# A bidirectional scan and a binary matmul on one core: stores at the end of late steps, whole low halves, and four small scalings moved

## The reference, cut to what matters

```python
# x, k: (4, 1024, 1024) float32; k serves as key and value; cond: (4, 256); weight: (1024, 1024)
tf = sigmoid(sum(cond, -1))[:, None, None]
decay = exp(-exp(w))[None, :] * (0.5 + 0.5 * tf[:, :, 0])
ek = exp(minimum(k, 30)); ekv = ek * k
# over time, forward and then in reverse:
#   a = a * decay + ekv[t] (nf, nb);  b = b * decay + ek[t] (df, db)
euk = exp(minimum(u + k, 30))
num = nf + nb - ekv + euk * k
den = df + db - ek + euk
y = sigmoid(x) * (num / maximum(den, 1e-8)) * (0.8 + 0.2 * tf)
bw = where(weight >= 0, 1, -1) * mean(abs(weight), axis=1, keepdims=True)
out = x + einsum('bsi,oi->bso', y, bw) + bias
```

## Time and profile before

| what | value |
|---|---|
| median of 3 runs | 494.87 us (494.64 to 496.08) |
| the profiled execution | 495.54 us, span 493.8 us from first to last instruction |
| VectorE busy | 472.8 us, 96% of the span |
| ScalarE busy | 403.3 us, 82% |
| GpSimd busy | 384.2 us, 78% |
| TensorE busy with products | 353.6 us, 72% |
| stores L372 | 24, median 8.8 us from issue to landing |

### The profile page before, as it was taken

The page is one execution under the profiler, slowest core; times in us unless marked ns, Lnnn a source line. Parts: engine busy times, 40 slices in busy tenths (PEclk is TensorE's granted clock), DMA queues, the critical chain, the costliest instruction groups (busy, mean ns, idle before and its releaser), DMA issues.

```text
span 493.8 us, 5418 instructions
## 1 busy us (share of the span) xinstructions
PE 353.6 (72%) x1803; PEld 212.2 (43%) x1803; DVE 472.8 (96%) x345; ACT 403.3 (82%) x451; POOL 384.2 (78%) x225
## 2 busy tenths in 40 slices
PE   3433453533348797797799698778869998899995
PEld 2332353433334454454355355434435554444442
DVE  5999999999999999999999999999999999999695
ACT  3977898998989879989998998999978878884600
POOL 0057877969787876988899698798998889899385
PEclk9976666656669998899899899989979999999999
DMA  7898799999987669799999967989879769777478
GB/s 215 224 282 274 179 278 292 297 305 288 249 210 180 175 154 171 152 207 212 200 193 184 231 134 154 241 157 213 160 123 149 122 115 133 103 159 124 53 122 220
DMA packets 101284, 94.23 MB, mean 191 GB/s; under 512 B 2924, under 2 KB 93064, under 8 KB 100744
## 3 DMA queue, kind: packets, MB, share of 16 engines
q0 software_dynamic: 31440, 36.18, 47.3%
q1 hardware_dynamic: 67720, 56.65, 36.6%
q10 hardware_dynamic: 2096, 1.05, 0.8%
HBM read 60.31 MB, written 37.75 MB: 199 GB/s over the span
## 4 chain that ended last, share of the span: by engine, by line
POOL 38%; ACT 24%; issue 23%; PE 13%; DVE 1%; DMA 0%; SPq 0%; POOLq 0%; ACTq 0%; DVEq 0%
POOL wkv L396 13%; POOL acts L360 5%; POOL out_dram L372 5%; POOL wkv L404 4%; POOL wkv L379 4%; POOL terms L407 4%; PE sT L525 3%; ACT x_nat L846 3%; POOL acts L354 3%; PE prod L525 3%; ACT rec L721 3%; ACT terms L686 2%; ACT euk L690 2%; PE kT L525 2%; ACT L849 2%
## 5 line engine op out<-in xcount | busy, mean ns | idle before, releaser
L484 PE MATMUL prod<-acts,sgn 128*128 128x512 f16 x752 | 176.2, 389 | 0.0
L966 DVE TENSOR_TENSOR_SCAN terms<-cols,y_start,terms 128x1024 f32<-128x1024 f32 x64 | 147.0, 2337 | 1.1
L952 DVE TENSOR_TENSOR_SCAN terms<-cols,terms 128x1024 f32<-128x1024 f32 x64 | 142.8, 2270 | 0.0
L484 PEld LDWEIGHTS prod<-acts,sgn 128*128 128x128 f16 x752 | 75.4, 100 | 83.4 <-issue 8.2
L396 POOL TENSOR_TENSOR wkv<-euk,rec 128x1024 f32<-128x1024 f32 x31 | 83.6, 2696 | 27.3 <-ACT rec L723 27.2
L379 POOL TENSOR_TENSOR wkv<-wkv,terms 128x1024 f32<-128x1024 f32 x31 | 74.7, 2408 | 27.7 <-DVE wkv L999 27.7
L404 POOL TENSOR_TENSOR wkv<-wkv,rec 128x1024 f32<-128x1024 f32 x31 | 78.1, 2518 | 1.2 <-ACT wkv L807 1.2
L455 PE MATMUL sT<-ident,x_nat 128*128 128x128 f32 x208 | 36.4, 333 | 40.4 <-DVE wkv L999 29.6
L360 POOL TENSOR_TENSOR acts<-wkv,rec 128x512 f16<-128x512 f32 x30 | 42.3, 1410 | 15.4 <-DVE euk L1008 15.0
L455 PE MATMUL kT<-ident,k_nat 128*128 128x128 f32 x248 | 41.3, 321 | 14.0 <-DVE own L983 14.0
L407 POOL DMA_DIRECT2D terms<-own x32 | 34.1, 1066 | 20.8 <-DVE terms L966 20.2
(11 more groups left out here) (124 smaller groups left out, 603.9 us busy)
## 6 DMA issues: line engine op xcount, KB each, us to landing
terms<-own POOLq DMA_DIRECT2D x32, 512.0 KB, 5.8
out_dram<-in_x_dram SPq DMA_DIRECT2D x32, 512.0 KB, 7.5
k_nat<-in_fside_BxSxS_dram SPq DMA_DIRECT2D x30, 512.0 KB, 6.7
x_nat<-in_x_dram SPq DMA_DIRECT2D x26, 512.0 KB, 4.9
out_dram<-o_nat POOLq DMA_DIRECT2D x24, 512.0 KB, 8.8
y_fm<-in_L_ffn_weight_dram SPq DMA_DIRECT2D x8, 512.0 KB, 8.2
out_dram<-in_L_ffn_bias_dram POOLq DMA_DIRECT2D x8, 512.0 KB, 8.2
x_end<-in_x_dram SPq DMA_DIRECT2D x6, 512.0 KB, 8.0
```

Of the source, the lines that this page charges most:

```text
L484: ins = pe.matmul(made_in(u), view[:, c, m % CT * P:m % CT * P + P], acts[:, part, m // CT % 2 * CT + c, h * H:(h + 1) * H], start=(part = ...
L952: dve.tensor_tensor_scan(buf, d, buf, 0.0, ALU.mult, ALU.add).then_inc(st["F" + kind], 1)
L966: dve.tensor_tensor_scan(buf[:, ::-1], d, buf[:, ::-1], y_start[:, i:i + 1], ALU.mult, ALU.add)\
```

## The change

From step 25 on GpSimd issues all stores of a step at its end. The low halves handled in steps 26, 27 and 28 are one instruction each and no longer two. In step 8 ScalarE's four scalings L788 stand behind `two`(7), where they stood ahead of `halves`(6). Which store is due in which step stays as it was, and nothing else is moved.

```diff
--- before.py
+++ after.py
@@ -89,7 +89,7 @@
         return 2 <= n < LAST and n % 3 == 1
 
     def split(n):
-        return hurried(n) or 2 <= n <= CT or LAST + 2 <= n < N - 3
+        return hurried(n) or 2 <= n <= CT
 
     def ends(n):
 
@@ -383,7 +383,7 @@
                 ready = summed(n)
                 if low:
                     base(n - 2)
-                if n < N - 1 and n != LAST + 1:
+                if n <= LAST:
                     for m in ready[0:1]:
                         store(m)
                     ready = ready[1:]
@@ -780,14 +780,6 @@
                     done(act, "base", n - 2)
                     halves(n - 2, p)
                 sooner = cleared(n - 1) if n == LAST + 2 else min(made(n - 1), cleared(n - 1) + 1)
-                if not wt and not late:
-
-                    done(act, "abs", CT - 1)
-                    act.wait_ge(s_gain, 1)
-                    for b in range(B):
-                        ins = act.activation(oscale[:, b * CT:(b + 1) * CT], asum[:, :], ACT.Identity,
-                                             scale=gain[:, b:b + 1])
-                    ins.then_inc(s_osc, 1)
                 if late and n < N - 2 and not hasty:
                     clear(cleared(n - 1), sooner)
                 if n == LAST:
@@ -806,6 +798,14 @@
                     done(act, "chk", n - 1)
                     act.activation(wkv[1 - p][:, :], wkv[1 - p][:, :], ACT.Copy,
                                    scale=-HI_SCALE * LO_GAIN, bias=2.0 * HI_SCALE * LO_GAIN).then_inc(st["two"], 1)
+                if not wt and not late:
+
+                    done(act, "abs", CT - 1)
+                    act.wait_ge(s_gain, 1)
+                    for b in range(B):
+                        ins = act.activation(oscale[:, b * CT:(b + 1) * CT], asum[:, :], ACT.Identity,
+                                             scale=gain[:, b:b + 1])
+                    ins.then_inc(s_osc, 1)
                 if n == LAST:
                     act.preload_act_table_set("natural_log_exp_and_others")
                 if late and hasty:
```

## The result

The changed kernel takes 492.46 us in the median of 5 runs (492.16 to 493.03). The kernel before, in 5 runs beside it, takes 495.04 us (494.64 to 496.81). The ratio is 0.994, with a 95% interval of 0.992 to 0.996: 2.6 us or 0.5% less. Forecast were 491.7 us, in a range of 490.9 to 493.5. So it became faster as forecast, but the sum was 0.6 us too large.

A forecast was written before the change was run, and what follows sets the result against it. VectorE's summed instructions were taken to bound the 32 steps, TensorE the last stage. TensorE's 2.75 us plus 0.45 from step 8 gave 3.2 us, covered by VectorE's 2.85 plus slack: 494.87 to 491.7 us, range 490.9 to 493.5.

The forecast's parts named there:

- What holds `den`: Claim: in steps 8, 28 and 29 a still running GpSimd multiply holds VectorE's `den`, stretching it by 0.72, 0.79 and 1.87 us.
- The landing of store 16: Store issued behind L407 in step 27 lands 8.9 us after L407 starts; ScalarE's copy of unit 40 stands some 2.7 us.
- Step 28: VectorE's `den` still starts against GpSimd's `inv`(27), but comes free earlier: -0.53 us.
- t: Time at which store 16 lands, between 403.3 and 405.6 us, taken as 403.8; `inv`(27) ends at t+7.45.
- Step 29: VectorE's `den` is free of GpSimd's `inv` for every landing time in the range: -1.87 us.
- Step 8: With the scale rows behind `two`, GpSimd's `low` and `inv` and VectorE's `den` end earlier: -0.45 us.
- From step 9 on everything hangs on VectorE's own instructions, so the 0.45 should last to the end: VectorE after step 8: the 0.45 us gained there should last to the end.
- the prediction's own signs of being wrong: `den`(29) stays stretched, store 16 takes over 10.7 us from L407, or `val` in a step begins to wait for exps.
- TensorE's chain: Last stage: chain to the transposition at 433.03 starts 2.95 us earlier; `own`(31) limits this to 2.75, with step 8 3.2.
- The sum: VectorE gains 0.45+0.53+1.87 = 2.85 us; with TensorE's last stage the whole kernel gains 3.2 us.
- the late landing: Rival: store 16 lands later, each us costing one in step 28; chance 0.12 for 0 to 1.4 us left, 0.04 slower.
- Descriptor generation: Rival: it holds `den`, not the multiply; moved stores cost up to 3 us in steps 27 to 30, 501 us; chance 0.03.

## Why the prediction was right, and where it was too large

- **What holds `den`**: right, and now tried with an instruction added for it.
- **The landing of store 16**: forecast 8.9 us behind the start of L407, measured 8.8 in both profiles. The idle time of ScalarE was 3.21 us, forecast 2.7.
- **Step 28**: forecast -0.53, measured -0.11 in the first profile and +0.13 in the second; this term failed. The formula was right: t+7.45 gives 404.49+7.45 = 411.94 for the end of `inv`, measured 409.52+2.36 = 411.88. The mis-sized term is t. L407 started at 395.69 and not at 394.9, for two reasons: the whole step was 0.20 late by step 24, and `low`(25) waited 0.71 us for ScalarE, which had itself waited 0.72 us for the product of unit 38 (387.67 above). The prediction had taken the run from `base` to `inv` as unbroken, from step 25, and had not asked whether ScalarE's queue would have its inputs when GpSimd got ahead. With store 16 at its old place (whole halves alone) the run takes from 385.45 to 396.38, 10.93 us; in the changed kernel it takes from 385.65 to 395.73, 10.08. So taking 1.58 us of store out of the way shortened it by only 0.85. In the second profile step 24 took nothing, `low`(25) waited 0.92 us instead, L407 started at 395.34 and t was 404.18; the sum needed L407 to move forward with the 0.45 us of step 8, to about 394.45.
- **Step 29**: forecast -1.87, measured -1.88, and free at both t of the changed kernel, as said; at t = 407.2, beyond the stated range, `den`(29) took 1.66 us.
- **Step 8**: forecast -0.45, measured -0.47. exps(9) ended at 132.32+1.09 = 133.41, forecast 133.3.
- **"From step 9 on everything hangs on VectorE's own instructions, so the 0.45 should last to the end"**: this step failed. ScalarE's copies also hang on the landing of stores, and the landing did not come earlier though VectorE did. Behind the wait for store 11 step 24 lost 0.61 us. The prediction looked at this kind of wait for the stores that the change moves, and not for those that it leaves. The second profile of the changed kernel (13.92 between the two `val`) shows that not every execution pays it there; that one lost in step 28 instead. `val`(25) waited 0.16 us for `exps`, one of the prediction's own signs of being wrong, in the first profile of the changed kernel and not in the second.
- **TensorE's chain**: forecast 3.2, measured 2.19 (2.51 in the second profile). The missing 1.0 is step 24 (0.61) and step 28 (0.42) again. `own`(31) does not limit it in the changed kernel; with the halves alone, when TensorE gets further ahead, it does, by 0.19 us.
- **The sum**: VectorE 2.85 forecast, 1.85 measured between steps 8 and 31 (2.15 in the second profile). The medians are 2.6 us apart in the first set of runs and 2.2 in the second, against 3.2; the result lies in the range because the largest term, step 29, held. That span and median moved by more than TensorE's 2.19 lies in the landing of the last stores, 4.28 and 3.06 us in the two profiles.
- **The part that pays**: the prediction costed the whole halves and the moved stores together and gave neither a price of its own. Alone, the whole halves give 3.1 us, the scale rows 0.3, which is not clear of noise, and the stores lose 1.3 to 1.7. Had the halves been worked out with the stores where they were, it would have shown that the move of the stores has nothing left to bring.
- **The rivals**: the late landing was the right one to fear; 2.7 us more of it make the kernel slower than before. Descriptor generation does not hold `den`: in step 27 two stores run beside it (396.29 to 399.73) and it takes 1.23 us.

## What to carry to other kernels

When a transfer is moved later to free its engine, find who waits for its landing, and on which engine's queue, before counting the freed time; here that wait cost what the move brought and more. A shift of the bound engine lasts only past places where the others do not wait for a DMA or for one another, so such waits with less than a microsecond of cover belong in the sum, even in steps that the change does not touch. And cost each part of a change with the others left out: two remedies for one lateness do not add up.

## What was not expected of the hardware

- The same store takes 8.5 to 11.5 us to land, and in these profiles the long times (10.6 and more) stand where the load of x is issued within 0.1 us of it and the short ones (8.5 to 9.1) where it comes 0.9 to 1.2 us after. When it is issued went with TensorE's granted clock in that stretch, 1.00 and 0.76 to 0.78. This goes together and was not tried.
- In one execution TensorE going idle for 2.25 us instead of 0.93 was followed by a lower granted clock (0.70 in the mean of 429 to 432 us), and its next eight products took 1.5 us longer on a chain without slack. Being early was no gain there.
- From the last VectorE instruction to the end of the last stores it takes 3.1 to 4.9 us in executions with the same last instructions, a difference as large as the effects that were looked for.
- A multiply of an input with itself, read as a repeated 128x128 tile into 16 bits, takes GpSimd 1.85 us, where one of two full 128x1024 tiles takes 2.32.
